# A graph network's edge loop that takes the nodes' end along, 46 of 49 pairs of node tiles

## The chip, the cores and the metric
One core of one Trainium2 chip. The metric is device time in microseconds of one execution. The core's engines are PE (matrix products), DVE (vector), ACT (scalar functions), POOL and SP; SP only issues DMAs here, and POOL issues indirect ones (gathers).

## The reference
12500 nodes of 64 values and 412500 edges, sorted by destination (400000 random ones in both directions and one loop a node, 33 edges a node on the average). Cut to what matters:
```python
x = layernorm(x + mean_over_neighbours_3_times(x))
xs, xr = x[src], x[dst]
flux_send = einsum(mlp_flux(xs).reshape(E, 64, 2), nvec)
flux_recv = einsum(mlp_flux(xr).reshape(E, 64, 2), nvec)
a = mlp_a((xs + xr) * 0.5)            # 3 hidden layers with relu, linear, layernorm
flux = 0.5 * (flux_send + flux_recv) - 0.5 * a * (xs - xr)
x = layernorm(x + (x + segment_sum(flux, dst)))
```

## The kernel before
The program runs in stages: preparation (find_nodes), three averaging layers (first_layer, later_layers), node_rows, which computes for each node what depends on the node alone and writes it as a row of 260 values (node_table, T5: x, y, the two flux rows), the edge loop (edge_pass), and the nodes' end (finish).

**The edge loop** takes 1024 edges a step (HE; 8 tiles of 128, TL), 403 steps (HS), with buffers in rings of 8 (RB). POOL gathers the sources' rows, one indirect DMA for a tile of 128 edges, 8 a step (L1635). ACT takes y out of the rows (L1721), PE turns it (L1652, L1655) and runs the layers, ACT applies relu, DVE and ACT the norm, and PE sums by destination (L1686 to L1695): each half step of 512 edges falls into a window of at most 32 nodes, with the last node's partial sum carried over. ACT copies the sums out (L1750), SP stores them to node_sums (ACC) in HBM (L1596), each store waiting for the one before it to land. A step is a software pipeline written out by hand: in the same step c each engine works on chunks c, c - 1, ... c - 5. DVE's step is spread(c) (edge_sel_t and three edge_sel, the selections) and then scale(c - 5) (edge_zx, edge_ssq, edge_sel_r). ACT's ends with root(c - 4), the square root for which the reciprocal and edge_sel_r of DVE's step c + 1 wait. SP's step is: a store of chunk c - 8, a wait for PE's turn of chunk c - 4, the loads of step c (edge_et with the indices, L1605, for POOL and DVE; edge_near, L1607; two edge_yd, L1609), and the other store of chunk c - 8. The order on each engine's queue is the order in which this code is written; nothing is scheduled by a planner. chunks() writes 11 steps in a row and then a loop of 8 steps a turn, 49 turns.

**The end** (finish) works on 98 tiles of 128 nodes in 7 groups of 14 (JG, NG). SP loads the four sums and the node's own row of a group (L1865, L1867, two buffers), DVE combines them in 13 operations (L1895 to L1910) and normalises (layer_norm, L1292 to L1299, with a root on ACT, L1880), SP writes the group out (L1871, L1873). It starts when the edge loop has ended on all engines.

## Time and profile before
| | us |
|---|---|
| median of 3 runs | 7836.83 (7833.52 to 7843.65) |
| the profiled execution | 7838.55 |
| its span | 7836.7 |
| PE, DVE, ACT, POOL busy | 5910.6, 3335.9, 2816.6, 5380.7 |
| edge loop, first to last gather | 3494.6 to 7615.0 |
| the end, first issue to the span's end | 7663.2 to 7836.7 |

The page's slices show the stages: the averaging layers up to 3400 us, with PE and POOL busy; from there the edge loop, in which POOL stands at 7 tenths and DVE at 3 to 4; in the last slice DVE alone. Read a share of busy time by stage only, and for POOL look also at the idle time before its instructions: POOL's issuing of a gather counts as busy, what lies between two of them doesn't.

### The profile page before, as it was taken

How to read it: one execution, taken by the hardware profiler on the slowest of the kernel's cores; microseconds unless marked ns; L12 is line 12 of the kernel's file. 1: busy time of each engine (PE TensorE's matmuls, PEld its weight loads, DVE VectorE, ACT ScalarE, POOL GpSimd, SP SyncE). 2: the span in 40 equal slices, each digit the busy share in tenths (PEclk: the TensorE clock that was granted, in tenths of full speed). 3: DMA queues.
4: the chain of work that ended last, by engine and by line, in shares of the span. 5: the costliest groups of instructions: out<-in, count | busy, mean ns of one | idle time of the engine just before them, and what ended most of it. 6: DMA issues, size and time to landing. Idle time of an engine off the chain costs nothing. (4 is left out here: it accounts for less than half of the span.)

```text
span 7836.7 us, 213920 instructions
## 1 busy us (share of the span) xinstructions
PE 5910.6 (75%) x80407; PEld 4886.7 (62%) x80407; DVE 3335.9 (43%) x6012; ACT 2816.6 (36%) x5153; POOL 5380.7 (69%) x5216
## 2 busy tenths in 40 slices
PE   0159999999999999757777777777777777777770
PEld 0159999989999999524555555555555555555550
DVE  5469989952221111463333333333333333333337
ACT  0168888850000000113444333343333434433440
POOL 5776766647776777217777777777777777777760
PEclk9999999999999999768888888888888888888885
DMA  5234434346665566325555555555555555555545
GB/s 118 73 114 146 145 129 145 130 176 226 215 228 212 206 216 219 114 86 132 137 138 136 136 136 137 137 137 136 136 136 137 138 136 137 137 136 136 137 120 153
DMA packets 647894, 1155.36 MB, mean 147 GB/s; under 512 B 396199, under 2 KB 454503, under 8 KB 629524
## 3 DMA queue, kind: packets, MB, share of 16 engines
q0 software_dynamic: 217440, 521.49, 26.8%
q1 hardware_dynamic: 419168, 593.46, 23.1%
q10 hardware_dynamic: 10212, 25.35, 1.0%
q8 instruction: 765, 12.53, 0.6%
q14 instruction: 309, 2.53, 0.1%
HBM read 931.86 MB, written 207.96 MB: 145 GB/s over the span
## 5 line engine op out<-in xcount | busy, mean ns | idle before, releaser
L1635 POOL DMA_INDIRECT edge_rows<-node_table,edge_et x3224 | 3137.7, 973 | 983.0 <-issue 944.6
L798 POOL DMA_INDIRECT two_rows<-x_parts,src_at x1120 | 1085.3, 969 | 477.8 <-issue 371.9
L1079 PE MATMUL two_acc<-x_parts,two_win 128*128 128x192 bf16 x16072 | 1355.8, 247 | 32.2 <-DMA two_win<-adjacency 16.8
L1079 PEld LDWEIGHTS two_acc<-x_parts,two_win 128*128 128x128 fp8e4 x16072 | 1340.8, 99 | 35.8 <-issue 33.6
L1822 DVE TENSOR_TENSOR edge_zx<-edge_zp,edge_rows 128x512 f32<-128x512 f32 x403 | 278.9, 692 | 2142.3 <-ACT edge_z L1734 2086.5
L1663 PE MATMUL edge_mp<-edge_h,edge_W 128*128 128x512 f32 x1612 | 1124.7, 837 | 0.0
L978 ACT ACTIVATE one_win<-one_count 128x784 fp8e4<-128x784 f32 x1312 | 1073.8, 824 | 135.2 <-PE one_count L939 63.9
L798 POOL DMA_INDIRECT one_rows<-x_parts,src_at x560 | 834.8, 1491 | 335.1 <-PE one_edge_acc L1002 170.4
L1721 ACT ACTIVATE edge_yc<-edge_rows 128x512 f32<-128x512 f32 x403 | 254.0, 630 | 2213.0 <-DMA edge_rows<-node_table,edge_et 2213.0
L1695 PE MATMUL edge_seg<-edge_seg,edge_edge_now 128*1 128x66 f32 x6448 | 292.4, 228 | 839.9 <-ACT edge_seg L1750 839.2
L925 PE MATMUL one_acc<-x_parts,one_win 128*128 128x192 bf16 x8036 | 858.5, 246 | 0.5 <-ACT one_win L978 0.5
L1686 PE MATMUL edge_seg<-edge_rows,edge_sel 128*32 128x66 f32 x6448 | 795.7, 222 | 1.3 <-DVE edge_sel_r L1828 1.2
L1690 PE MATMUL edge_seg<-edge_rows,edge_sel 128*32 128x66 f32 x6448 | 787.4, 221 | 0.0
L1688 PE MATMUL edge_seg<-edge_z,edge_sel_r 128*32 128x66 f32 x6448 | 766.7, 233 | 0.0
L1687 PE MATMUL edge_seg<-edge_rows,edge_sel 128*32 128x66 f32 x6448 | 766.7, 233 | 0.0
L1689 PE MATMUL edge_seg<-edge_zx,edge_sel_r 128*32 128x66 f32 x6448 | 766.6, 233 | 0.0
L1652 PE MATMUL edge_tp<-ident,edge_yc 128*128 128x128 f32 x1612 | 529.3, 349 | 280.7 <-issue 197.6
L939 PE MATMUL one_count<-one_high,one_low 128*128 128x196 bf16 x5248 | 677.4, 250 | 52.2 <-DVE one_high L910 24.6
L1695 PEld LDWEIGHTS edge_seg<-edge_seg,edge_edge_now 128*1 128x1 f32 x6448 | 128.0, 81 | 895.1 <-ACT edge_seg L1750 893.7
L925 PEld LDWEIGHTS one_acc<-x_parts,one_win 128*128 128x128 fp8e4 x8036 | 685.3, 97 | 1.1 <-issue 0.7
L1663 PEld LDWEIGHTS edge_mp<-edge_h,edge_W 128*128 128x128 f32 x1612 | 394.1, 270 | 319.7 <-issue 319.5
L910 DVE TENSOR_TENSOR one_high<-values,one_slot 128x3136 bf16<-128x3136 bf16 x328 | 585.2, 1784 | 0.0
(289 smaller groups left out, 10477.3 us busy)
## 6 DMA issues: line engine op xcount, KB each, us to landing
two_win<-adjacency SPq DMA_DIRECT2D x82, 3136.0 KB
adjacency<-one_win SPq DMA_DIRECT2D x41, 3136.0 KB
edge_near<-near_ids SPq DMA_DIRECT2D x403, 192.0 KB
edge_rows<-node_table,edge_et POOLq DMA_INDIRECT x3224
node_sums<-edge_seg SPq DMA_DIRECT2D x806, 33.0 KB
two_rows<-x_parts,src_at POOLq DMA_INDIRECT x1120
end_sums<-node_sums SPq DMA_DIRECT2D x7, 1848.0 KB
edge_yd<-y_parts SPq DMA_DIRECT2D x806, 12.0 KB
```

The lines of the kernel that those rows point to most:

```text
L798: pool.indirect_dma_start(rows[:, b % 2, i * GB + d, :], None, XP.rearrange("p (j c) -> (p j) c", c=3 * C), bass.IndirectOffsetOnAxis(ap=s ...
L925: mm = pe.matmul(acc[h.b2][:, half * 3 * C:(half + 1) * 3 * C], win[:, h.b2, half, j, :].bitcast(FP8), now[:, j, :], start=(j == 0), stop= ...
L939: mm = pe.matmul(to, low[:, k, 2 * g + i // 2, :, i % 2], high[:, k, 2 * g + i // 2, :, i % 2], start=True, stop=True)
L978: act.activation(to, count[s % 2][:, :, 0:4 * J].rearrange("p b (n v) -> p v b n", n=2), ACT.Copy, saturate=True).then_inc(taken, 1)
L1079: mm = pe.matmul(acc[b][:, half * 3 * C:(half + 1) * 3 * C], win[:, b, half, j, :].bitcast(FP8), now[:, j, :], start=(j == 0), stop=(j == ...
L1635: pool.indirect_dma_start(rows[:, h.b, t, :], None, T5, bass.IndirectOffsetOnAxis(ap=et[:, h.b, 0, t:t + 1].bitcast(I32), axis=0))\
L1663: pe.matmul(mp[i - 1][:, :], W[:, i - 1, :], hT[i - 1][:, h.b % 2, :], start=True, stop=True)\
L1686: pe.matmul(into(0), sel[:, h.b, 1, t, :], row[:, X_F0:X_F0 + W6], start=first, stop=False, tile_position=(0, 0))
L1687: pe.matmul(into(1), sel[:, h.b, 0, t, :], row[:, 0:W6], start=first, stop=False, tile_position=(0, NW))
L1688: pe.matmul(into(2), sel_r[:, h.b % 2, t, :], z[:, h.b % 2, t, :], start=first, stop=False, tile_position=(0, 2 * NW))
L1689: pe.matmul(into(3), sel_r[:, h.b % 2, t, :], zx[:, h.b % 2, t, :], start=first, stop=False, tile_position=(0, 3 * NW))
L1690: pe.matmul(into(0), sel[:, h.b, 2, t, :], row[:, X_F1:X_F1 + W6], start=False, stop=False, tile_position=(0, 0))
```

## The change
Most tiles of nodes are complete long before the edge loop ends, since the edges are sorted by destination. The change moves the end of 92 of the 98 tiles into the loop, as 46 pairs, one pair per turn of 8 steps.

SP, ACT and DVE now write 35 steps in a row (chunks with more = 3), and their loop has 46 turns; PE and POOL keep 11 steps and 49 turns. In the loop, a pair goes through the 8 steps ("turn" 0 to 7) thus. SP in turn 0: loads the pair's sums and own rows, behind the step's second store. DVE in turns 1, 2 and 3: 4, 4 and 5 operations of combine, on 128 columns; in turn 4 mean, difference, squares and their sum. ACT in turn 5: a square root. DVE in turn 6: reciprocal and product. SP in turn 7: waits for these and writes 256 rows out. DVE's part stands at the end of its step, behind edge_sel_r, and ACT's behind its last root. Pair k is loaded when the stores of chunks up to 26 + 8k have landed. find_nodes gets a test that pair k's edges end before the step 27 + 8k (four small operations and an addition); where they don't, the program takes its general path, which also serves other unusual inputs. finish handles the last 6 tiles in two groups of 3. Two broadcast loads (the norm's factors) come ahead of two others in the edge loop's set-up on SP.

```diff
+DONE_LAG = 3
+DONE = (HS - RB - (HS - RB) % RB - DONE_LAG * RB) // RB
+DONE_PEEL = RB + (HS - RB) % RB + DONE_LAG * RB
+JE = (J - 2 * DONE) // 2
...
-def chunks(eng, body, total=CH, ring=NB):
-
-    peel = ring + (total - ring) % ring
+def chunks(eng, body, total=CH, ring=NB, more=0):
+
+    peel = ring + (total - ring) % ring + more * ring
...
+            pool.iota(done_by[:, :], pattern=[[RB * HE, DONE]], base=(DONE_PEEL - RB) * HE, channel_multiplier=0,
...
+            o.link(dve.tensor_tensor(late, start[0:1, 2:2 * DONE + 2].rearrange("p (k i) -> p k i", i=2)[:, :, 0], done_by[:, :], ALU.subtract))
+            o.link(dve.tensor_reduce(span_gap[:, 0:1], late, AX, ALU.max))
+            o.link(dve.tensor_scalar(span_gap[:, 0:1], span_gap[:, 0:1], 0.0, None, ALU.is_gt))
+            o.link(dve.tensor_copy(late[:, 0:1], span_gap[:, 0:1]))
...
+            sp.dma_start(alw_b[:, :], alw.partition_broadcast(P)).then_inc(L, 16)
+            sp.dma_start(alb_b[:, :], alb.partition_broadcast(P)).then_inc(L, 16)
...
+                if not early(h, DONE_PEEL):
+                    turn = (h.place - DONE_PEEL) % RB
+                    if turn == 0:
+                        sp.wait_ge(sems["stored"], (h.c - BACK) * 2 * 16)
+                        sp.sem_inc(sems["storing"], 1)
+                        sp.wait_ge(sems["done_used"], h.r + 1)
+                        sp.sem_inc(sems["storing"], 1)
+                        sp.dma_start(node_sums[:, :, :, :].rearrange("p j k c -> p j (k c)"),
+                                     ACC.rearrange("(j p) k c -> p j (k c)", p=P)[:, bass.ds(2 * h.r, 2), :]).then_inc(sems["done_in"], 16)
+                        sp.dma_start(own[:, :, :], T5.rearrange("(j p) c -> p j c", p=P)[:, bass.ds(2 * h.r, 2), :]).then_inc(sems["done_in"], 16)
+                    elif turn == 7:
+                        sp.wait_ge(sems["done_made"], h.r + 1)
+                        sp.sem_inc(sems["storing"], 1)
+                        sp.dma_start(out[bass.ds(2 * P * h.r, 2 * P), :].rearrange("(j p) c -> p j c", p=P), res[:, :, :]).then_inc(sems["done_out"], 16)
+            chunks(sp, step, HS, RB, DONE_LAG)
             for c in range(HS - BACK, HS):
                 for u in range(2):
                     store(Chunk(0, c, RB), u)
             sp.wait_ge(sems["stored"], 2 * HS * 16)
+            sp.wait_ge(sems["done_out"], DONE * 16 + 16)
...
+                if not early(h, DONE_PEEL) and (h.place - DONE_PEEL) % RB == 5:
+                    act.wait_ge(sems["done_squares"], h.r + 1)
+                    act.activation(done_stat[:, :], done_stat[:, :], ACT.Sqrt, bias=eps4_col[:, 0:1], scale=1.0 / C)\
+                        .then_inc(sems["done_rooted"], 1)
 
             stages = ((1, lambda h: relu(h, 0)), (2, lambda h: relu(h, 1)), (3, lambda h: relu(h, 2)), (4, squares), (5, take), (4, root))
-            chunks(act, step, HS, RB)
+            chunks(act, step, HS, RB, DONE_LAG)
...
+            oc = Chain(dve, sems["order_c"])
+
+            def done(h, turn):
+
+                x1 = own[:, :, 0:C]
+                wide = lambda col: col.broadcast_to([P, 2, C])
+                each = lambda rw: rw.unsqueeze(1).broadcast_to([P, 2, C])
+                own_cnt = cnt[:, bass.ds(2 * h.r, 2)].unsqueeze(2)
+                if turn == 1:
+                    oc.at(h.r * 20)
+                    dve.wait_ge(sems["done_in"], 32 * h.r + 32)
+                    dve.wait_ge(sems["done_out"], 16 * h.r + 16)
+                    oc.link(dve.tensor_tensor(res[:, :, :], own[:, :, X_F0:X_F0 + C], wide(node_sums[:, :, 0, C:C + 1]), ALU.mult))
+                    oc.link(dve.tensor_tensor(mix[:, :, :], own[:, :, X_F1:X_F1 + C], wide(node_sums[:, :, 0, C + 1:C + 2]), ALU.mult))
+                    oc.link(dve.tensor_tensor(res[:, :, :], res[:, :, :], node_sums[:, :, 0, 0:C], ALU.add))
+                    oc.link(dve.tensor_tensor(res[:, :, :], res[:, :, :], mix[:, :, :], ALU.add))
+                elif turn == 2:
+                    oc.link(dve.tensor_tensor(mix[:, :, :], x1, node_sums[:, :, 2, 0:C], ALU.mult))
+                    oc.link(dve.tensor_tensor(mix[:, :, :], node_sums[:, :, 3, 0:C], mix[:, :, :], ALU.subtract))
+                    oc.link(dve.tensor_tensor(mix[:, :, :], mix[:, :, :], each(alw_b[:, :]), ALU.mult))
+                    oc.link(dve.tensor_tensor(res[:, :, :], res[:, :, :], mix[:, :, :], ALU.subtract))
+                elif turn == 3:
+                    oc.link(dve.tensor_tensor(mix[:, :, :], x1, wide(own_cnt), ALU.mult))
+                    oc.link(dve.tensor_tensor(mix[:, :, :], node_sums[:, :, 1, 0:C], mix[:, :, :], ALU.subtract))
+                    oc.link(dve.tensor_tensor(mix[:, :, :], mix[:, :, :], each(alb_b[:, :]), ALU.mult))
+                    oc.link(dve.tensor_tensor(res[:, :, :], res[:, :, :], mix[:, :, :], ALU.subtract))
+                    oc.link(dve.scalar_tensor_tensor(res[:, :, :], x1, 4.0, res[:, :, :], ALU.mult, ALU.add))
+                    dve.sem_inc(sems["done_used"], 1)
+                elif turn == 4:
+                    spread_of = lambda col: col.unsqueeze(2).broadcast_to([P, 2, C])
+                    oc.link(dve.tensor_reduce(done_mean[:, :], res[:, :, :], AX, ALU.add))
+                    oc.link(dve.tensor_scalar(done_mean[:, :], done_mean[:, :], 1.0 / C, None, ALU.mult))
+                    oc.link(dve.tensor_tensor(res[:, :, :], res[:, :, :], spread_of(done_mean[:, :]), ALU.subtract))
+                    oc.link(dve.tensor_tensor(done_sq[:, :, :], res[:, :, :], res[:, :, :], ALU.mult))
+                    oc.link(dve.tensor_reduce(done_stat[:, :], done_sq[:, :, :], AX, ALU.add))
+                    dve.sem_inc(sems["done_squares"], 1)
+                elif turn == 6:
+                    spread_of = lambda col: col.unsqueeze(2).broadcast_to([P, 2, C])
+                    dve.wait_ge(sems["done_rooted"], h.r + 1)
+                    oc.link(dve.reciprocal(done_stat[:, :], done_stat[:, :]))
+                    oc.link(dve.tensor_tensor(res[:, :, :], res[:, :, :], spread_of(done_stat[:, :]), ALU.mult))
+                    dve.sem_inc(sems["done_made"], 1)
+
             def step(h):
                 spread(h)
                 if not early(h, LAG):
                     scale(h.back(LAG))
-            chunks(dve, step, HS, RB)
+                if not early(h, DONE_PEEL):
+                    done(h, (h.place - DONE_PEEL) % RB)
+            chunks(dve, step, HS, RB, DONE_LAG)
...
+    JG, NG, J0 = JE, 2, 2 * DONE
...
-        res = sb("res", [P, J, C])
+        res = sb("res", [P, J - J0, C])
...
+                js = slice(J0 + g * JG, J0 + (g + 1) * JG)
...
```

**DVE, end of a step in the loop.** Before, edge_sel_r (L1828) is followed by the next step's selections:
```order
L1827 RECIPROCAL edge_ssq<-edge_ssq 128x8
L1828 TENSOR_TENSOR edge_sel_r<-edge_sel,edge_ssq 128x256
L1803 REGISTER_ALU
L1804 TENSOR_SCALAR edge_sel_t<-edge_near,edge_node_of 96x1024
L1809 TENSOR_TENSOR edge_sel<-edge_ramp,edge_et 128x256
L158 REGISTER_ALU
L1810 TENSOR_TENSOR edge_sel<-edge_sel,edge_et 128x256
L1811 TENSOR_TENSOR edge_sel<-edge_sel,edge_et 128x256
```
After, in turn 2, the pair's four operations stand between (L1870 is L1828 of before, L1846 is L1804):
```order
L1869 RECIPROCAL edge_ssq<-edge_ssq 128x8
L1870 TENSOR_TENSOR edge_sel_r<-edge_sel,edge_ssq 128x256
L1890 TENSOR_TENSOR edge_mix<-edge_own,edge_node_sums 128x128
L163 REGISTER_ALU
L1891 TENSOR_TENSOR edge_mix<-edge_node_sums,edge_mix 128x128
L163 REGISTER_ALU
L1892 TENSOR_TENSOR edge_mix<-edge_mix,edge_alw 128x128
L163 REGISTER_ALU
L1893 TENSOR_TENSOR edge_res<-edge_res,edge_mix 128x128
L163 REGISTER_ALU
L1845 REGISTER_ALU
L1846 TENSOR_SCALAR edge_sel_t<-edge_near,edge_node_of 96x1024
```
edge_sel_t and the three edge_sel of the next step come behind the pair's operations; the step's delivery to PE, edge_sel_r, stays ahead of them.

**SP, end of a step in the loop.** Before, the second store of a step (L1596) is followed by the next step's first:
```order
L1585 ISA
L1585 TENSOR_LOAD edge_base_i
L1585 ISA x2
L1596 ISA
L1596 DMA node_sums<-edge_seg 4x32x66
L1589 ISA
L1594 REGISTER_ALU
```
After, in turn 0, two loads stand between:
```order
L1605 ISA
L1605 TENSOR_LOAD edge_base_i
L1605 ISA x2
L1616 ISA
L1616 DMA node_sums<-edge_seg 4x32x66
L1637 REGISTER_ALU
L1639 ISA
L1639 DMA edge_node_sums<-node_sums 128x2x264
L1641 ISA
L1641 DMA edge_own<-node_table 128x2x260
L1609 ISA
L1614 REGISTER_ALU
```
The next step's store and its loads, edge_et among them, come behind these. In turn 7 the output of the pair stands in the same place, behind a wait for DVE.

**DVE, the end.** Before, the groups have 896 columns (14 tiles of 64):
```order
L1885 MEMSET end_eps_col 128x1
L1895 TENSOR_TENSOR end_res<-end_own,end_sums 128x896
L1896 TENSOR_TENSOR end_am<-end_own,end_sums 128x896
L1897 TENSOR_TENSOR end_res<-end_res,end_sums 128x896
L1898 TENSOR_TENSOR end_res<-end_res,end_am 128x896
```
After, 192 (3 tiles):
```order
L1973 MEMSET end_eps_col 128x1
L1983 TENSOR_TENSOR end_res<-end_own,end_sums 128x192
L1984 TENSOR_TENSOR end_am<-end_own,end_sums 128x192
L1985 TENSOR_TENSOR end_res<-end_res,end_sums 128x192
L1986 TENSOR_TENSOR end_res<-end_res,end_am 128x192
```
The operations of a group and their order are the same; there are 2 groups instead of 7.

## Rows read from the trace of the kernel before

**Rows 1.** Busy time by stretch: stretch, its length, each engine, clock, DMA
```profile
3700.00:7600.00 3900.00, 2894.23 (x46199) 2056.39 (x46197) 1365.11 (x3429) 1559.10 (x3434) 2969.63 (x3052) 0.84 0.56 137
7663.00:7836.00 173.00, 0.00 (x0) 0.00 (x0) 140.43 (x141) 2.15 (x7) 0.00 (x0) 0.50 0.56 171
```
**Rows 2.** Groups by line, 3700 to 7600 us: count, busy us, mean ns, idle before
```profile
L1635 POOL DMA_INDIRECT edge_rows<-node_table,edge_et x3052 | 2969.9, 973 | 930.6 <-issue 893.7 <-DMA edge_et<-edges_turned 28.4 <-PE edge_seg L1695 8.5
...
L1828 DVE TENSOR_TENSOR edge_sel_r<-edge_sel,edge_ssq 128x256 f32<-128x256 f32 x381 | 162.5, 426 | 13.1
L1810 DVE TENSOR_TENSOR edge_sel<-edge_sel,edge_et 128x256 f32<-128x256 f32 x381 | 162.0, 425 | 13.1
L1811 DVE TENSOR_TENSOR edge_sel<-edge_sel,edge_et 128x256 f32<-128x256 f32 x381 | 161.8, 425 | 0.0
...
L1809 DVE TENSOR_TENSOR edge_sel<-edge_ramp,edge_et 128x256 f32<-128x256 f32 x381 | 157.0, 412 | 0.0
```
**Rows 3.** Waits, 3700 to 7600 us: us in total, times, longest
```profile
ACT edge_yc L1721 <- DMA edge_rows<-node_table,edge_et: 2043.2, 382, 8.0
DVE edge_zx L1822 <- ACT edge_z L1734: 1962.9, 363, 8.4
...
PEld edge_tp L1652 <- issue: 270.0, 329, 5.3
...
SPq L1590 <- ACT edge_seg L1750: 541.4, 228, 5.1
```
**Rows 4.** The gathers' line, 3700 to 7600 us: ns least/middle/most
```profile
L1635 POOL DMA_INDIRECT edge_rows<-node_table,edge_et x3052: 946/950/1525, 3699.7 to 7599.0; - x191
```
**Rows 5.** Timeline of POOL and DVE: start, us, what, idle before
```profile
5511.99 1.10 POOL L1635 DMA_INDIRECT edge_rows<-node_table,edge_et  x1 [0.30 <-issue]
...
5517.17 0.95 POOL L1635 DMA_INDIRECT edge_rows<-node_table,edge_et  x1 [0.30 <-issue]
...
5519.69 0.96 POOL L1635 DMA_INDIRECT edge_rows<-node_table,edge_et  x1 [0.30 <-issue]
...
5512.16 0.42 DVE L1809 TENSOR_TENSOR edge_sel<-edge_ramp,edge_et 128x256 f32<-128x256 f32 x1
...
5517.53 0.69 DVE L1822 TENSOR_TENSOR edge_zx<-edge_zp,edge_rows 128x512 f32<-128x512 f32 x1 [4.15 <-ACT edge_z L1734]
...
5526.27 0.42 DVE L1828 TENSOR_TENSOR edge_sel_r<-edge_sel,edge_ssq 128x256 f32<-128x256 f32 x1
```
**Rows 6.** Groups by line, 900 to 1900 us, the first averaging layer
```profile
L798 POOL DMA_INDIRECT one_rows<-x_parts,src_at x349 | 509.9, 1461 | 226.1 <-PE one_edge_acc L1002 125.1 <-issue 100.9
...
L910 DVE TENSOR_TENSOR one_high<-values,one_slot 128x3136 bf16<-128x3136 bf16 x208 | 371.2, 1785 | 0.0
...
L909 DVE TENSOR_TENSOR one_low<-values,one_slot 128x2048 bf16<-128x2048 bf16 x207 | 252.9, 1222 | 45.5 <-PE one_count L939 38.0 <-DVE x_parts L883 5.7 <-issue 0.4
```
**Rows 7.** The chain that ended last, then the timeline, from 7663 us on
```profile
7664.53 13.88 DMA end_own<-node_table
...
7678.53 1.09 DVE L1895 TENSOR_TENSOR end_res<-end_own,end_sums 128x896 f32<-128x896 f32 x1 [15.23 <-DMA end_own<-node_table]
...
7699.89 1.09 DVE L1895 TENSOR_TENSOR end_res<-end_own,end_sums 128x896 f32<-128x896 f32 x1
...
7828.04 0.37 SPq L1871 DMA_DIRECT2D out<-end_res  x1
```
**Rows 8.** Timeline of the edge loop's set-up, DVE and SP
```profile
3491.95 0.22 DVE L1012 TENSOR_TENSOR edge_bo_rest<-edge_bo_rest,edge_bo_parts 128x64 f32<-128x64 f32 x1
...
3479.95 0.59 SPq L1580 DMA_DIRECT2D edge_bo<-in_L_gnn_a_bo  x1
```
**Rows 9.** Timeline of SP's queue: in the loop, and the tail
```profile
5507.81 0.36 SPq L1605 DMA_DIRECT2D edge_et<-edges_turned  x1
...
5525.09 4.91 SPq L1596 DMA_DIRECT2D node_sums<-edge_seg  x2
...
7640.16 20.15 SPq L1596 DMA_DIRECT2D node_sums<-edge_seg  x7
```

More of the change, by code:

```diff
@@ L97 @@
 assert GC % GB == 0 and BLKS == DP - 1 and DP % 2 == 1 and BLKS % 2 == 0 and PARTS == 5
+DONE_LAG = 3
+DONE = (HS - RB - (HS - RB) % RB - DONE_LAG * RB) // RB
+DONE_PEEL = RB + (HS - RB) % RB + DONE_LAG * RB
+JE = (J - 2 * DONE) // 2
+assert 0 < DONE < PAIRS - 1 and J == 2 * DONE + 2 * JE
 CLEARS = 101
@@ L212, in build_program @@
                        cnt, has, rcnt, end_idx, start_idx, beyond, src_at, near_at)
-        general = nc.values_load(beyond[0:1, 0:1], min_val=0, max_val=4 * P)
+        general = nc.values_load(beyond[0:1, 0:1], min_val=0, max_val=5 * P)
         with nc.If(general == 0):
@@ L458, in find_nodes @@
         tile_low = sb("tile_low", [P, 2 * HQ])
+        done_by, late = sb("done_by", [1, DONE]), flat[0:1, 4 * 2 * HQ * GC:4 * 2 * HQ * GC + DONE]
         e_dst, e_src = sb("e_dst", [RR, 2, HE], I32), sb("e_src", [RR, 2, HE], I32)
@@ L517, in _ @@
         def _(pe):
-            pe.wait_ge(consts, 5)
+            pe.wait_ge(consts, 6)
             for k in range(4):
@@ L744, in _ @@
             o.link(dve.tensor_scalar(past[0:1, :], past[0:1, :], float(SPAN), None, ALU.is_gt))
+            o.link(dve.tensor_tensor(past[0:1, :], past[0:1, :], late[:, 0:1], ALU.add))
             for b in range(2):
@@ L1555, in edge_pass @@
         bh = sb("bh", [P, 3])
+        node_sums, own = sb("node_sums", [P, 2, 4, W6]), sb("own", [P, 2, W5])
+        res, mix, done_sq = sb("res", [P, 2, C]), sb("mix", [P, 2, C]), sb("done_sq", [P, 2, C])
+        done_stat, done_mean, eps4_col = sb("done_stat", [P, 2]), sb("done_mean", [P, 2]), sb("eps4_col", [P, 1])
+        alw_b, alb_b = sb("alw", [P, C]), sb("alb", [P, C])
         tp, zp = ps("tp", [P, 4 * P]), ps("zp", [P, TL, C])
@@ L1611, in step @@
                     store(h.back(BACK), 1)
-            chunks(sp, step, HS, RB)
+                if not early(h, DONE_PEEL):
[13 more added lines that the diff above has]
+            chunks(sp, step, HS, RB, DONE_LAG)
             for c in range(HS - BACK, HS):
@@ L1868, in _ @@
             for g in range(NG):
-                whole = min(JG, J - 1 - g * JG)
+                whole = min(JG, J - J0 - 1 - g * JG)
                 sp.wait_ge(done, g + 1)
-                sp.dma_start(out[g * JG * P:(g * JG + whole) * P, :].rearrange("(j p) c -> p j c", p=P),
+                sp.dma_start(out[(J0 + g * JG) * P:(J0 + g * JG + whole) * P, :].rearrange("(j p) c -> p j c", p=P),
                              res[:, g * JG:g * JG + whole, :]).then_inc(stored, 16)
-            sp.dma_start(out[(J - 1) * P:N, :], res[0:N_LAST, J - 1, :]).then_inc(stored, 16)
+            sp.dma_start(out[(J - 1) * P:N, :], res[0:N_LAST, J - J0 - 1, :]).then_inc(stored, 16)
             sp.wait_ge(stored, 16 * (NG + 1))
@@ L1887, in _ @@
             for g in range(NG):
-                b, js = g % 2, slice(g * JG, (g + 1) * JG)
+                b, js = g % 2, slice(J0 + g * JG, J0 + (g + 1) * JG)
                 dve.wait_ge(brought[b], 32 * (g // 2 + 1))
-                sm, ow, h = sums[:, b, :, :, :], own[:, b, :, :], res[:, js, :]
+                sm, ow, h = sums[:, b, :, :, :], own[:, b, :, :], res[:, g * JG:(g + 1) * JG, :]
                 x1 = ow[:, :, 0:C]
```

16 lines of the change are left out of this document (10 added, 6 removed).

## The prediction
> **What bounds the kernel now.** I read the busy time of the last two stages first [rows 1]. Between 3700 and 7600 us, inside the edge loop, POOL is busy 2970 of 3900 us and everybody else less (DVE 1365, ACT 1559). Behind 7663 only DVE works, 140 of 173 us: that is the nodes' end, 2.2% of the span. Next the loop's groups by line [rows 2]: POOL issues 3052 gathers of 973 ns, and its idle time before them is 931 us, 305 ns apiece, almost all of it "issue", so it waits for nothing that the profile shows. Sum: 2970 + 931 = 3901 us, the whole stretch. POOL sets the loop's pace: 8 gathers a step, 8 x 1.278 = 10.22 us, and 403 steps make the 4.12 ms. The waits confirm it from the other side [rows 3]: ACT waits 2043 us for gathered rows and DVE 1963 us for ACT, 5.2 us of each 10.2 us step; SP's queue waits 541 us for ACT, 1.4 us a step. So the question is twofold: what the 173 us of the end shrink to, and what the work taken along costs POOL.
>
> **What disturbs POOL.** A gather takes 946 ns at least, 950 in the middle and 1525 at most [rows 4]. The excess over the least is 2970 - 3052 x 0.946 = 83 us, 0.22 us a step. The timeline says who it is [rows 5]: the gather at 5511.99 has the DVE operation of 5512.16 on top of it, and the two that follow it, of two SBUF inputs each, and takes 1.10 us; the one at 5517.17, beside the 0.69 us operation that reads one input from PSUM (edge_zx), takes 0.95. The stretch of the first layer shows the same effect large: there the gathers take 1461 ns in the mean, beside two-input operations of 1785 and 1222 ns [rows 6]. The mechanism as I read it: a gather that reads its indices from SBUF while DVE has two SBUF inputs waits until the DVE operation ends.
> The Trainium skill ("SBUF — State Buffer", Who interferes with whom) says that a DVE instruction with two SBUF inputs contends with a GpSimd instruction that reads SBUF; by that rule these waits are expected, and the 1.10 us beside 0.95 us agrees.
>
> **The change part by part.**
> *Removed: the end on DVE.* A group of 14 tiles starts at 7678.53 and the next at 7699.89 [rows 7]: 21.36 us, seven of them 149.5 us, up to the last output's issue at 7828.04. Each has 16 two-input operations (12 of combine, the one with the factor 4, 3 of the norm) of 1.09 us, 1.126 with the step to the next; two reductions of about as much; and 21.36 - 18 x 1.126 = 1.09 us of small ones and the turn to ACT. After it there are two groups of 3 tiles, 192 columns. An operation takes 0.22 us at 64 columns [rows 8], 0.41 to 0.43 at 256 [rows 2] and 1.09 at 896 [rows 7], a straight line of about 1.04 ns a column: 0.354 us at 192, 0.39 with the step. A group: 18 x 0.39 + 1.09 = 8.1 us, two 16.2. **Saved: 149.5 - 16.2 = 133.3.**
> *The end's load.* The first group's rows land at 7678.41, 13.9 us behind their issue [rows 7], with 3.8 MB each for this group and the one behind it under way. Of 3 tiles it is 0.8 MB a group: at the rate seen (3.8 MB in 14 us) 3 us of transfer. The tail's stores follow one another at (20.15 - 0.6) / 6 = 3.26 us, each waiting for the landing of the one before [rows 9], so a latency is below that, an estimated 2 us. I take 5 instead of 14. **Saved: 9** (8 to 11). The last output is smaller too: **0.5** (0 to 2).
> *Added before the loop.* Two broadcast loads on SP ahead of those for which DVE waits, 0.59 us each by the row of a like one [rows 8]: **+1.2**, as POOL's first gather waits for that set-up. Four small operations of the test and an addition in the node search, on DVE, some 0.2 us each: **+0.8** (0 to 1.2). The iota on POOL is under 0.2 us, beside DMAs.
> *Added in the loop, 46 times in 8 steps.* DVE gets 16 two-input operations of 128 columns, 0.29 us each by the line above (4.6 us), two reductions, a scaling and a reciprocal (together 1 us): 5.6 us in 81.8, at most five or six operations and 1.7 us in one step. They stand behind edge_sel_r, where the step's product for PE is already delivered, and ahead of the next selections. DVE waits 5.2 us a step for ACT [rows 3], so their own time costs nothing; without that cover it would be 46 x 5.6 = 258 us. What they cost is POOL's wait. The four two-input operations of a step take 643 us in the stretch [rows 2], 1.69 us a step, and go with 0.22 us of excess: 0.13 us a us. In proportion the new ones cost 4.64 x 0.13 = 0.60 us an iteration; if both the chance to meet a reading gather and the wait grow with the operation's length (0.29 against 0.42), 0.41. The bounds: nothing, if POOL gets its turn in the gaps between short operations; and the ratio of the first layer, where operations are four times as long: (1461 - 946) x 349 = 180 us over 371 + 253 us of DVE [rows 6], 0.29, which makes 1.34 us an iteration, 62 us. I take 0.5, near the row of like length: **+23** (0 to 62).
> *ACT* gets one square root of 2 columns behind its own root, under 1 us by any row, in a step in which it waits 5.2 us for rows: **0**.
> *SP, and who waits behind it.* In turn 0 two loads of 270 KB, each 0.4 to 1 us to issue, behind the step's second store; in turn 7 a wait for DVE and an output of 64 KB. What is queued behind that wait is the next step's store and then edge_et, for which POOL waits. How early is edge_et? The one issued at 5507.81 serves the step whose first gather starts at 5519.69 [rows 9, 5]: 12 us ahead. SP follows PE's turns, and PE is up to 5.3 us late at its branch [rows 3], so some 6.6 us are left at worst, of which landing takes 2 to 3. How late can SP become? It starts its step's last store at 5525.09 and is free at 5525.7; DVE's edge_sel_r of the step before ends at 5526.69 [rows 5], and the pair's last two operations, of turn 6, would end 0.55 us later, at 5527.2; the output's issue takes it to 5528. The row of the two stores ends at 5530.00, so the next store started near 5529.4, with an estimated microsecond of register work ahead of it. So SP is late by 0 to 2 us once in eight steps, and 1.4 us of idle time a step win it back: **0** (0 to 10). The loads' 540 KB may hold gathers and stores by some 2 to 4 us, by the rate above; gathered rows are needed by ACT, and PE's sums free a buffer more than a step before POOL wants it.
> *The tail.* SP's chain of stores is the last thing before the end: seven stores in 20.15 us from 7640.16 [rows 9]. SP enters the tail some 5 us later by the wait in turn 7; the first stores of the tail still go at POOL's pace of 10.2 us for two, against 6.5 us of their own, so this is won back: **0** (0 to 3).
> *The head.* On SP, ACT and DVE 35 steps instead of 11 stand in a row before the loop proper; it is the same work, and each of them waits in every step: **0**.
>
> **The sum.** -133.3 - 9 - 0.5 + 1.2 + 0.8 + 23 = -117.8. The profiled execution has 7836.7 of span and 7838.55 in all, 1.7 above the median of 7836.83; in its own terms the span goes to 7718.9, and on the median it is 7836.8 - 117.8 = **7719**.
>
> **The rivals.**
> 1. *POOL is blocked for the whole of each new operation* (ends on the other side). The place is the index read of the gathers, the price 4.64 us an iteration. If a gather could not go on at all while a two-input operation runs, 46 x 4.64 = 213 us would be added: 7836.8 - 142.8 + 2 + 213 = **7909**. It decides from 142.8 - 2 = 141 us on, 3.06 us an iteration, that is 0.66 us of POOL's time per us of DVE's. Against it: the loop shows 0.13 and even the first layer 0.29. The Trainium skill (the same section) says that whoever comes second is fully blocked until the first has finished; the wait is then the rest of one operation, not its whole length, unless the read always comes at its start. By that rule read strictly the time would be this rival's. For it: the new operations come as chains with 35 ns between them, so that a gather could meet two in a row. Chance 4%.
> 2. *SP starves POOL.* If the wait in turn 7, or the 540 KB ahead of the stores, puts edge_et later than POOL's start, each us of it counts 46 times. With 1 us an iteration the time is 7719 + 46 = **7765**. For it: PE's 5.3 us at the branch, less 3 of landing, leave a lead of only 4. Against: that delay reaches DVE two steps behind the branch (edge_sel_t waits for the turn two steps back), in turn 2, and not in turn 6, for which SP waits. Chance 7%.
> 3. *The work in the loop costs nothing on POOL*: **7696**. For it: POOL wins the gaps. Against: even isolated operations cost it now. Chance 12%.
> 4. *The change does not do what it says*: the new test sends the program down the general path. Pair k needs its last edge by step 27 + 8k; at 33 edges a node it ends at 8448 (k + 1), against 1024 (27 + 8k): for k = 45 388608 against 396288. The margin of 7680 edges is far more than random edges scatter. Chance 1%, at a time far above all ranges.
>
> **How the numbers follow.** The forecast, with 0.3 to 0.8 us an iteration (7710 to 7733), has 76%. With rival 3 and most of rival 2 the range is 7692 to 7762: the lower end is rival 3 with the load's best case and a little of the last output, the upper one the first layer's ratio (7719 + 39 = 7758) and some us of SP. 0.2% are 15.7 us, about what a measurement of this kernel tells from no change. Faster by over 0.2% needs less than 2.7 us an iteration: 94%. Within 0.2%: 1%. Slower: 5% (rivals 1 and 4).
>
> **What would show each step.** Behind the loop: two groups of about 8 us on DVE with operations of 0.35 us, and the first landing 5 us behind its issue. In the loop: POOL's gathers with a mean of 980 to 987 ns instead of 973, the slow ones under the new edge_res and edge_mix operations, 10.25 to 10.35 us a step, and no idle time of POOL for edge_et. SP should wait for DVE 1 to 4 us in turn 7. I am wrong if POOL shows idle time before a gather that ends with edge_et (rival 2), if gathers beside the new operations are slowed by 0.3 us or more each time (rival 1), or if the tail's seven stores take longer than 20 us.

## The result, and the profile after

The changed kernel takes 7723.11 us (median of 4 runs, 7712.23 to 7734.1) against 7835.18 us of the kernel before on the same chip (4 runs, 7819.5 to 7843.65): ratio 0.9859, interval 0.9838 to 0.9881, faster by 1.4%. The forecast was 7719, in a range of 7692 to 7762. The profiled execution of the changed kernel took 7727.65 us, its span 7722.8 us, 113.9 us shorter than the span before.

First the two stretches of [rows 1], after; the columns are the same, and the second stretch is now 57 us long instead of 173:
```profile
3700.00:7600.00 3900.00, 2885.31 (x45874) 2059.58 (x45873) 1598.10 (x4325) 1561.23 (x3458) 2973.75 (x3034) 0.83 0.58 143
7663.00:7720.00 57.00, 11.69 (x377) 10.13 (x373) 19.56 (x56) 6.64 (x19) 0.00 (x0) 0.65 0.14 39
```
In the loop DVE has 233 us more in 3900, and POOL issued 18 gathers fewer in the same time. Behind the loop 20 us of DVE are left of 140.

The groups by line of the same stretch, the counterpart of [rows 2]:
```profile
L1670 POOL DMA_INDIRECT edge_rows<-node_table,edge_et x3034 | 2974.9, 981 | 926.6 <-issue 888.4 <-DMA edge_et<-edges_turned 32.3 <-PE edge_seg L1730 5.8
...
L1846 DVE TENSOR_SCALAR edge_sel_t<-edge_near,edge_node_of 96x1024 bf16<-96x1024 bf16 x379 | 194.0, 512 | 417.0 <-PE edge_tp L1690 257.5 <-DMA edge_near<-near_ids 115.7 <-DVE edge_done_stat L1907 15.4
...
L1851 DVE TENSOR_TENSOR edge_sel<-edge_ramp,edge_et 128x256 f32<-128x256 f32 x379 | 155.9, 411 | 0.0
...
L1898 DVE TENSOR_TENSOR edge_res<-edge_res,edge_mix 128x128 f32<-128x128 f32 x45 | 13.1, 292 | 1.5
...
L1885 DVE TENSOR_TENSOR edge_res<-edge_own,edge_node_sums 128x128 f32<-128x128 f32 x46 | 13.1, 285 | 0.0
```
A gather takes 981 ns in the mean instead of 973, POOL's idle time is still "issue", 305 ns apiece, and its wait for edge_et is 32 us against 28. The new operations take 0.285 to 0.292 us (0.29 forecast). New is edge_sel_t's wait for edge_near, 116 us. The gathers' line shows the least and the middle as in [rows 4]; only the slow ones grew in number:
```profile
L1670 POOL DMA_INDIRECT edge_rows<-node_table,edge_et x3034: 946/954/1547, 3699.6 to 7599.8; - x190
```

Then the end, as in [rows 7]: SP's last stores of the loop and the end's loads, DVE's first operation of each of the two groups, and the outputs.
```profile
7632.50 57.41 SPq L1616 DMA_DIRECT2D node_sums<-edge_seg  x16
...
7694.19 0.49 SPq L1955 DMA_DIRECT2D end_own<-node_table  x1
...
7699.78 0.36 DVE L1983 TENSOR_TENSOR end_res<-end_own,end_sums 128x192 f32<-128x192 f32 x1 [6.83 <-DMA end_own<-node_table]
...
7707.79 8.46 SPq L1959 DMA_DIRECT2D out<-end_res  x2
7707.85 0.36 DVE L1983 TENSOR_TENSOR end_res<-end_own,end_sums 128x192 f32<-128x192 f32 x1
...
7716.29 0.46 SPq L1961 DMA_DIRECT2D out<-end_res  x1
```

With these starts the 113.9 us fall into six parts. The first and the last gather, and the end's first issue on SP (7663.16 and 7692.82), are read from the timelines.

| part of the span | before | after | difference | forecast |
|---|---|---|---|---|
| up to the first gather | 3494.6 | 3497.4 | +2.8 | +2.0 |
| first to last gather | 4119.5 | 4144.6 | +25.1 | +23 |
| last gather to the end's first issue | 49.1 | 50.9 | +1.8 | 0 |
| that issue to DVE's first operation | 15.4 | 7.0 | -8.4 | -9 |
| DVE's groups, to the last output's issue | 149.5 | 16.5 | -133.0 | -133.3 |
| the rest | 8.7 | 6.5 | -2.2 | -0.5 |

So the saving is where it was expected, and 25 of 144 us are given back in the loop. Which mechanism takes them is the open question: the new operations themselves, as the forecast's term says, or the operations behind them, which they push back.

**Who makes the gathers late.** A gather with nothing in its way starts 1.25 us after the one before (0.95 and 0.30). For each gather after which the next is late by x (25 ns or more) I looked for a DVE operation that ends at its start + x + 0.12 us, within 25 ns. Nearly always there is exactly one, and I take it as the one the gather waited for. Summed over the steps of the loop proper (the 46 turns), smaller delays included, x is 81.4 us before and 105.8 after, +24.4, the loop's loss. By turn of the eight steps the rise is in two of them: turn 3 from 16.9 to 29.8 us, turn 4 from 10.2 to 19.5; all the others together 54.3 and 56.5. By the operation at whose end the wait ended (whole loop, us): the first edge_sel 30.5 before and 62.8 after, the second and third 24.7 and 23.4, edge_sel_r 9.6 and 7.3, edge_sel_t 6.3 and 2.6, all the new operations 3.4, in 43 gathers. This place shows both at once (DVE, then POOL):
```profile
4482.98 0.29 DVE L1905 TENSOR_TENSOR edge_res<-edge_res,edge_done_mean 128x128 f32<-128x128 f32 x1
4483.31 0.29 DVE L1906 TENSOR_TENSOR edge_done_sq<-edge_res 128x128 f32<-128x128 f32 x1
4483.63 0.29 DVE L1907 TENSOR_REDUCE edge_done_stat<-edge_done_sq 128x2 f32<-128x128 f32 x1
4484.26 0.48 DVE L1846 TENSOR_SCALAR edge_sel_t<-edge_near,edge_node_of 96x1024 bf16<-96x1024 bf16 x1 [0.34 <-DVE edge_done_stat L1907]
4484.66 0.42 DVE L1851 TENSOR_TENSOR edge_sel<-edge_ramp,edge_et 128x256 f32<-128x256 f32 x1
...
4483.14 0.95 POOL L1670 DMA_INDIRECT edge_rows<-node_table,edge_et  x1 [0.30 <-issue]
4484.39 1.50 POOL L1670 DMA_INDIRECT edge_rows<-node_table,edge_et  x1 [0.30 <-issue]
```
The gather at 4483.14 starts under the new operation of 4482.98, which ends 0.13 us later; two more start while it runs, and it takes its 0.95 us. The next one begins inside edge_sel_t, is not let in when that ends, and goes on only when the first edge_sel ends too, at 4485.08: it takes 1.50 us. edge_sel_t and the first edge_sel stand one behind the other with no gap, a block of 0.82 us. Gathers over 0.3 us late in the loop proper: 13 before, 87 after. The block of turn 4 falls near turn 3's last gather: in the mean it began 1.8 us ahead of that gather's start before the change and begins 0.25 us ahead after. The block of turn 5 began 1.1 us ahead of turn 4's last gather and now begins with it. 39% and 57% of these last gathers are over 0.3 us late now. The waits that end with the first edge_sel rise from 2.0 to 24.1 us at these two gathers, and from 2.3 to 11.7 us at the second and third gather of turn 3.

**What holds a gather.** The three traces before, after and light_gap (below) give the rule plainly. The second and third edge_sel, edge_sel_r and the new two-input operations were already running, for 0.05 us or more, at the start of 598 gathers and ended 0.16 us or more behind it: all 598 gathers were late, 590 of them by that end less 0.12 us, within 30 ns. 1265 times such an operation began 0 to 0.3 us behind a gather's start: not one gather waited for its end. So an operation holds a gather only if it already runs when the gather starts (or is joined to one that does, as below), and the gather loses the operation's rest less 0.12 us. An estimate from this, for gathers 1.25 us apart that meet the operations at random: the 736 new operations of 0.29 us cost 736 x (0.29 - 0.05 - 0.12)^2 / (2 x 1.25) = 4.2 us (3.4 measured); 403 blocks of 0.82 us that held to their end would cost 68 us.

The block does not always hold to its end. Of the gathers that began inside edge_sel_t (0.1 us or more after its start, 0.16 or more ahead of its end), 37 went on at edge_sel_t's own end in the trace before, and 11 at the first edge_sel's; after, it is 14 and 73. The latter cost 5.2 us before and 36.0 after, which is the whole rise at the first edge_sel. It goes by the turn: before, all of turns 0 and 5 (11) were held to the second end and none of the others (30 in the loop proper); after, all 25 of turns 3 and 4 are too. The row of [rows 5] that the prediction reads is of the first kind, as the line that is missing there shows:
```profile
5511.76 0.48 DVE L1804 TENSOR_SCALAR edge_sel_t<-edge_near,edge_node_of 96x1024 bf16<-96x1024 bf16 x1 [4.33 <-PE edge_tp L1655]
```
The gather of 5511.99 took 1.10 us, 0.15 more than the least, and that fits the end of edge_sel_t at 5512.24 less 0.12; the first edge_sel was already running by then. The two kinds have the same overlap of 80 ns between the two operations. In the looped steps of the eight traces without an added wait they separate by one thing: DVE's last register or semaphore instruction ahead of the first edge_sel ended up to 0.151 us after edge_sel_t's start in all 216 of the first kind, and 0.160 us or more after it in all 237 of the second. That is a correlation; no run varied it.

### The profile page after: what moved, and what is told of

Read it like the earlier page. It is cut to its first block and busy times, and to the rows that moved or that the text cites. A ratio compares the mean times of both kernels' runs of the same rounds, so it can differ in the third digit from the quotient of the medians.

```text
span 7722.8 us, 216276 instructions
## 1 busy us (share of the span) xinstructions
PE 5923.9 (77%) x80407; PEld 4903.8 (63%) x80407; DVE 3453.0 (45%) x6838; ACT 2827.7 (37%) x5194; POOL 5394.2 (70%) x5217
## 5 line engine op out<-in xcount | busy, mean ns | idle before, releaser
L1698 PE MATMUL edge_mp<-edge_h,edge_W 128*128 128x512 f32 x1612 | 1105.4, 824 | 0.0
L1687 PE MATMUL edge_tp<-ident,edge_yc 128*128 128x128 f32 x1612 | 556.2, 362 | 318.2 <-issue 234.3
```

The lines of the kernel that those rows point to most:

```text
L1698: pe.matmul(mp[i - 1][:, :], W[:, i - 1, :], hT[i - 1][:, h.b % 2, :], start=True, stop=True)\
```

## The experiments

Theories: A1, the new two-input operations cost POOL directly (the forecast's term); A2, they cost almost nothing, and the block edge_sel_t + edge_sel that they push is what costs; C, SP's lateness.

In four sets of runs every kernel took half as long again in all its stages, the kernel before too (11732 to 11895 us). Most of POOL's idle time is then a wait for edge_et, so the times of these runs can't test A1 against A2; only ratios within a set are used. The changed kernel as it stands is in none of them.

**no_sums, early, gap_after, gap_before** (one set; before 11872.91). no_sums keeps the pair's loads, waits, root and output in the loop and leaves out DVE's arithmetic, early moves done() between spread() and scale() and ACT's root to the start of its step, and gap lets the first edge_sel wait for edge_sel_t's end; gap_before is the kernel before with that wait.
```diff
 no_sums, in done():   - oc.link(dve.tensor_tensor(...))   (all operations of turns 1 to 6)
 early, DVE's step:      spread(h)
                       + if not early(h, DONE_PEEL): done(...)
                         scale(h.back(LAG))
                       - if not early(h, DONE_PEEL): done(...)
 gap:                  - o.at(base + h.c)
                       + o.at(base + 2 * h.c)
                       - dve.tensor_scalar(sel_t[...], near[...], ...)
                       + o.link(dve.tensor_scalar(sel_t[...], near[...], ...))
```


> Leaves the pair's arithmetic on DVE out of the loop (16 two-input operations, reductions, scaling, reciprocal); the loads, the waits, the square root on ACT and the output stay, so 92 tiles are written as zeros. First gather to last gather was 4119.5 us before and 4144.6 with the change. Theory A (the arithmetic's operations stand in POOL's way, themselves or by what they push back): the stretch falls to 4119 to 4124. Theory C (the 540 KB of loads and SP's lateness cost the time): it stays at 4138 to 4147. The time would be about 20 us below the changed kernel's by A, the same by C.

> The pair's part on DVE moves ahead of scale: it stands between spread (edge_sel_t and the three edge_sel) and edge_zx, in DVE's wait for ACT, so that it pushes edge_sel_t no longer back; the square root on ACT moves to the start of its step. The same 16 operations run. Theory A1 (the new operations themselves block gathers, 0.5 us an iteration): first to last gather stays near 4144, within 5. Theory A2 (they cost POOL next to nothing; the loss comes from edge_sel_t and the first edge_sel, pushed to a moment at which a gather starts, in turns 3 and 4): the stretch falls to 4120 to 4128, the time by 15 to 25 us.

> The changed kernel with one wait more in each step: the first edge_sel waits until edge_sel_t has ended, so that there is a gap of some 35 ns between the two. Theory A2: a gather that is held by edge_sel_t gets in at the gap instead of waiting for the end of the first edge_sel as well; of the 58 us that gathers wait up to that end now, some 40 go, and first to last gather falls from 4144.6 to 4100 to 4115. Theory A1: the gap changes nothing, 4140 to 4150.

> The kernel before with the same gap between edge_sel_t and the first edge_sel. Theory A2: of the 28 us that gathers wait up to the end of the first edge_sel in it, about 20 go: first to last gather from 4119.5 to 4096 to 4106. Theory A1: no change, 4117 to 4122.

Measured: no_sums 11634.31, 0.9801 [0.9768, 0.9834]; early 11757.47, 0.9898 [0.9882, 0.9915]; gap_after 11601.04, 0.9761 [0.9725, 0.9797]; gap_before 11878.05, 1.0001 [0.9992, 1.0011]. From first to last gather they have 6759.7, 6883.0, 6740.0 and 6873.3 us, where the kernel before had 4119.5 in its own trace. The groups by line between 5500 and 11000 us say why these times test no theory, first gap_before:
```profile
L1635 POOL DMA_INDIRECT edge_rows<-node_table,edge_et x2563 | 2448.1, 955 | 3052.4 <-DMA edge_et<-edges_turned 2336.7 <-issue 715.7
```
and no_sums, with no new arithmetic at all:
```profile
L1670 POOL DMA_INDIRECT edge_rows<-node_table,edge_et x2604 | 2502.1, 961 | 2996.8 <-DMA edge_et<-edges_turned 2096.2 <-issue 748.9 <-PE edge_seg L1730 98.0
```
POOL is idle for 3000 of 5500 us and waits 2100 to 2300 of them for edge_et, so a gather that is 0.3 us late need not cost anything. What holds there is the end: early has gap_before's loop (+9.7 us) and is 121 us faster, about what the end saved. no_sums and gap_after have a loop that is 114 and 133 us shorter than gap_before's. I have no reason that I could show for that. The single gathers do speak: in no_sums, with edge_sel_t and edge_sel joined, 23 of the 40 that began inside edge_sel_t were held to the first edge_sel's end, the longest took 1533 ns; in gap_after all 43 went on at edge_sel_t's end, and the longest took 1223.

**gap_after2 and early2** (two of these kernels again, in two further sets).


> Again the changed kernel with the gap between edge_sel_t and the first edge_sel, since in the first run of it the program took 1.5 times as long in all its stages, the kernel before too, and POOL was idle for half the loop. Where POOL is never idle, theory A2 expects first to last gather at 4100 to 4115 us instead of 4144.6, and about 30 us less time than the changed kernel (near 0.982 of the kernel before). Theory A1 expects no change: 4140 to 4150, 0.986.

> Again the kernel in which the pair's part on DVE stands between spread and edge_zx, to be read where POOL is never idle. Theory A2 (the 16 operations themselves cost POOL next to nothing, the pushed edge_sel_t does): first to last gather 4120 to 4128 us instead of 4144.6, ratio to the kernel before about 0.983. Theory A1 (the operations themselves block gathers): 4140 to 4150, ratio 0.986.

Measured: 11449.3, 0.9734 [0.9694, 0.9773], and 11601.59, 0.9881 [0.9865, 0.9898]: the slow pace again and the same two ratios.

**The light kernels.** PE does a quarter of its sums by destination (6 of 24 products a half step are left; the 9 of the expectation is a miscount), so that it can't be what sets the pace:
```diff
 in sums(h):   - for k in range(4):
               + for k in range(1):      (quarters 1 to 3 end at their first product)
               - for q in range(4):      (the carried row)
               + for q in range(1):
```
light_before is the kernel before with this edit, light_after the changed one, light_early and light_gap add the edits above to light_after. Their sums are incomplete, so they are only good for timing. One execution each, beside one of the kernel before of 7831.13: the usual pace was back for the whole kernel as well, and on a chip on which early2 had run at the slow one, so it is not the edit that brought it back.

> The kernel before with 9 of 24 products by destination left per half step (one edge tile of four is summed, and one of four carried rows added; the sums are therefore incomplete): in the earlier runs on this chip PE issued its products 1.4 us apart over half of each step and POOL waited. Both theories: with PE out of the way POOL sets the pace again, first to last gather 4100 to 4140 us, gathers at 1.25 us with some slowed. It is the base for the next three.

> The changed kernel with the same products left out. Both theories: the stretch is longer than light_before's by 10 to 30 us (25 in the whole kernels). They differ in which DVE operation's end the slowed gathers wait for: theory A1 expects the 16 new operations, theory A2 the first edge_sel behind edge_sel_t, in turns 3 and 4 of eight.

> The same with the pair's part on DVE between spread and edge_zx. Theory A2: within 6 us of light_before. Theory A1: as light_after.

> light_after with the gap between edge_sel_t and the first edge_sel. Theory A2: below light_after by 20 us or more, and below light_before as well. Theory A1: as light_after.

Measured, with waits by the operation at whose end they ended, as above (us, whole loop):

| | time | first to last gather | first edge_sel | edge_sel_t | new operations | gathers over 0.3 us late, loop proper |
|---|---|---|---|---|---|---|
| light_before | 7836.05 | 4117.9 | 32.8 | 7.0 | - | 25 |
| light_after | 7741.69 | 4165.1 | 83.7 | 2.5 | 5.8 | 133 |
| light_early | 7710.5 | 4136.1 | 36.9 | 4.4 | 5.8 | 19 |
| light_gap | 7683.62 | 4102.7 | 0 | 16.6 | 5.8 | 4 |

light_before repeats the kernel before (7836.05 and 4117.9 us of gathers), so POOL sets the pace here as there; without that the rest would say nothing. The change costs 47.2 us of loop here, where both theories expected 10 to 30, and the waits at the first edge_sel alone rise by 50.9. Of the 133 gathers over 0.3 us late, 74 are in turns 3 and 4, where A2 had them, but 24 in turn 1, where it had none. light_early has the same new operations and the same loads, and leaves the block about where it was: the loss falls to 18.2 us, the first edge_sel to 36.9. So where the pair's operations stand is 29 of 47 us, and A1 alone falls. But A2 had expected light_early within 6 us of light_before; 18 is a miss. Of the 18.2 us, 5.8 are waits that end with a new operation, 6.4 are delays under 25 ns that my reading gives to nobody, and 4.1 are at the first edge_sel; 5.1 of the 18.2 arise in the first 35 steps, where no pair is worked on. These are single executions, and four of the kernel before lie 24 us apart: the 18 us are not clear of that, the 29 barely, and it is the sort of the waits that bears the reading.

light_early changes a second thing. DVE's part comes earlier in its step, so that SP waits for it less in turn 7, and edge_et is issued 10.4 us ahead of turn 0's first gather in the mean, against 6.0 in light_after. By itself the pair light_after and light_early could not tell A2 from C. light_gap can: SP is as late in it as in light_after (6.3 us ahead), and its loop is the shortest.

light_gap breaks the block. Its groups by line between 3900 and 7600 us, POOL and the first edge_sel:
```profile
L1670 POOL DMA_INDIRECT edge_rows<-node_table,edge_et x2907 | 2812.3, 967 | 888.8 <-issue 852.3 <-DMA edge_et<-edges_turned 28.3 <-PE edge_seg L1730 8.2
...
L1851 DVE TENSOR_TENSOR edge_sel<-edge_ramp,edge_et 128x256 f32<-128x256 f32 x363 | 158.5, 437 | 29.9 <-DVE edge_sel_t L1846 19.7 <-issue 0.5 <-PE edge_seg L1730 0.2
```
against light_after:
```profile
L1670 POOL DMA_INDIRECT edge_rows<-node_table,edge_et x2861 | 2824.9, 987 | 875.4 <-issue 836.5 <-DMA edge_et<-edges_turned 27.7 <-PE edge_seg L1730 11.2
```
967 ns a gather instead of 987, less than the 973 of light_before, with all the new operations in place. The timeline shows the gap, 0.21 us between edge_sel_t and edge_sel (35 ns were expected), and gathers beside it at 1.04 and 1.13 us:
```profile
5288.79 0.48 DVE L1846 TENSOR_SCALAR edge_sel_t<-edge_near,edge_node_of 96x1024 bf16<-96x1024 bf16 x1 [0.33 <-DVE edge_done_stat L1907]
5289.48 0.42 DVE L1851 TENSOR_TENSOR edge_sel<-edge_ramp,edge_et 128x256 f32<-128x256 f32 x1 [0.21 <-DVE edge_sel_t L1846]
...
5289.05 1.04 POOL L1670 DMA_INDIRECT edge_rows<-node_table,edge_et  x1 [0.30 <-issue]
5290.40 1.13 POOL L1670 DMA_INDIRECT edge_rows<-node_table,edge_et  x1 [0.30 <-issue]
```
Over the whole loop the longest gather of light_gap is 1266 ns:
```profile
L1670 POOL DMA_INDIRECT edge_rows<-node_table,edge_et x3224: 946/955/1266, 3499.2 to 7601.9; - x190
```
That of light_after is 1547:
```profile
L1670 POOL DMA_INDIRECT edge_rows<-node_table,edge_et x3224: 946/950/1547, 3494.0 to 7659.1; - x190
```
The loop is 62.4 us shorter than light_after's and 15.2 shorter than light_before's, the program 58 us shorter. The sum closes: light_before less its 32.8 us at the first edge_sel, plus 9.6 more at edge_sel_t and 5.8 of new operations, is 4100.5; measured 4102.7. All 128 gathers that began inside edge_sel_t went on at its end, where it was 14 of 122 in light_after. The 62 us are well clear of the spread of single executions, the 15 are not; for them speaks only that the sum closes.

**gap_after3 and gaps_two** (one set; before 11894.88). gaps_two also breaks the second edge_sel from the third:
```diff
 - o.at(base + 2 * h.c)
 + o.at(base + 3 * h.c)
 - dve.tensor_tensor(sel[:, h.b, 1, :, :], ...)
 + o.link(dve.tensor_tensor(sel[:, h.b, 1, :, :], ...))
```


> The whole changed kernel with the gap between edge_sel_t and the first edge_sel, once more. The runs with fewer products gave 4165.1 us without and 4102.7 with the gap. Where POOL is never idle: theory A2 expects first to last gather 4095 to 4115 us instead of 4144.6, a time of about 7723 - 35 = 7688, ratio to the kernel before 0.981. Theory A1: 4140 to 4150, ratio 0.986.

> The same with a second gap, between the second and the third edge_sel, which now run in one block of 0.77 us. Theory A2: the waits up to the third one's end (about 9 us in all) mostly go; 4 to 10 us less than with one gap, ratio 0.980. Theory A1: no difference from the changed kernel.

Measured, at the slow pace once more: gap_after3 11589.33, 0.9748 [0.9732, 0.9765]; gaps_two 11603.15, 0.9759 [0.9737, 0.9781]. The second gap brings nothing there, where POOL is not what bounds the loop, so this does not test what was expected of it. The changed kernel with the gap has the lowest median in each set in which it ran, 2.4 to 2.7% under the kernel before, though its interval overlaps those of no_sums and gaps_two. At the usual pace the whole version was not run. The light pair says 58 us; as the waits at the first edge_sel are 62.8 us in the whole kernel against 83.7 in the light one, some 45 us is my estimate for it.

## Why the prediction came out

The time was right (7719 against 7723), and the terms of the end within a microsecond or two. The loop's term was right in its number and wrong in its cause: that it hit was luck.

- **The end.** Groups 8.07 us apart (8.1 forecast), operations of 0.36 us (0.354), 16.5 us in all (16.2): the straight line through 0.22 us at 64 columns, 0.41 at 256 and 1.09 at 896 held at 192. The load landed so that DVE began 7.0 us behind SP's first issue instead of 15.4; 8.4 saved, 9 forecast, the term that mixed a rate with an estimated latency. The rest gave 2.2 where 0.5 (0 to 2) was set, just outside.
- **The head.** +2.8 against +2.0: 1.2 up to the edge loop's first load, 1.6 in its set-up. Right in size.
- **The loop's term, +23.** It was written as 46 iterations x 4.64 us of new two-input operations x 0.11, as if any such operation cost POOL in proportion to its length. Measured is +25.1, of which waits at the new operations themselves are 3.4 us: 0.016 us per us of theirs (5.8 us and 0.027 in the light kernels). The other 21 come from where edge_sel_t and the first edge_sel now stand: +32.3 at the first edge_sel, and 11 less at the others and in small delays. The step that failed is "four two-input operations take 643 us and go with 83 us of excess, 0.13 a us": a mean over operations that stand alone and a block of two, and with edge_sel_t, the block's first, not counted. By the count and the estimate above the cost of an operation does not go with its length, but with the square of what it has beyond 0.17 us. The clue was in [rows 5]: the gather of 1.10 us was put down to the three edge_sel on top of it, but all three start behind it; what it waited for is edge_sel_t, which the rows leave out. The second clue, that DVE's order puts edge_sel_t behind the pair's operations, I had described and priced at nothing, "their own time costs nothing", because DVE has 5.2 us of idle time. That cover is real for DVE and PE; POOL is not under it. It cares when the block comes, not whether DVE has time.
- **Rival 1** (blocked for the whole of each operation, 7909): wrong, by 3.4 us instead of 213. The gather at 4483.14 takes 0.95 us under two new operations. By the Trainium skill ("SBUF — State Buffer", Who interferes with whom) whoever issues first holds the shared ports for the whole instruction and the other is fully blocked. For a gather that comes second the row of 4484.39 agrees, and so do the 598 above, with 0.12 us of the wait costing nothing. The other way round the runs differ: a new operation that starts while a gather runs is not held by it (0.290 us in the mean, 0.295 for those that start between gathers), nor does it hold the gather. That is why a chain of short operations on top of a gather costs it so little, as at 4483.14.
- **Rival 3** (no cost, 7696): wrong in the result, near in the mechanism. In light_gap, with a gap in the block, the loop is 15 us shorter than light_before's even with the new work in it, in one execution of each.
- **SP and rival 2.** The forecast was a delay of 0 to 2 us, won back at once. Worked out over all steps of the loop proper, edge_et's issue led its step's first gather by 9.8 to 11.5 us in every turn before; after it leads by 6.2, 6.4, 6.9, 7.8, 8.3, 9.4, 10.2 and 10.6 us in turns 0 to 7, 4.6 at least. So SP is 4.5 us late at turn 0 and needs the eight steps to win it back: size and recovery were both off. Its wait for DVE in turn 7 is 3.2 us, within the 1 to 4 of the forecast; but the next store starts 4.8 us behind the output's issue in the mean, where the forecast had 1.4. The wait (3800 to 7600 us), then the rows behind it (SP's queue, turn 7 and turn 0):
```profile
SPq L1644 <- DVEq L1914: 142.4, 45, 5.1
...
3928.18 0.44 SPq L1645 DMA_DIRECT2D out<-edge_res  x1
3933.23 0.68 SPq L1616 DMA_DIRECT2D node_sums<-edge_seg  x1
3934.34 0.36 SPq L1625 DMA_DIRECT2D edge_et<-edges_turned  x1
3938.94 0.65 SPq L1616 DMA_DIRECT2D node_sums<-edge_seg  x1
3940.01 0.41 SPq L1639 DMA_DIRECT2D edge_node_sums<-node_sums  x1
3940.65 0.39 SPq L1641 DMA_DIRECT2D edge_own<-node_table  x1
```
  The edge_et of 3934.34 serves the gathers from 3939.41 on, 5.1 us ahead, and landing is within that. POOL's wait for edge_et stays at 32 us, so rival 2 did not come. By the prediction's 2 to 3 us for landing, which no row shows, the least lead of 4.6 us leaves some 2 us to spare. DVE feels it first: edge_sel_t waits 116 us for edge_near, issued behind edge_et, mostly in turns 0 and 1, and begins 0.7 to 0.9 us later in them relative to the gathers. These have 3.7 us more of excess in the two turns (14.6 before, 18.3 after). So C is worth a few us at the most, and light_gap agrees.
- **The tail.** +1.8 against 0 (0 to 3); SP's last seven stores take 20.1 us, as before.

What stays open: why light_early keeps 18 us where the new operations account for 5.8; the share of placement in the full kernel, which rests on the reading of its trace and on the light pair, since no full run at the usual pace moved the block; what makes a gather slip in between edge_sel_t and the first edge_sel in some turns and not in others; and why at the slow pace the loops of no_sums and gap_after are some 120 us shorter than those of early and gap_before.

## What to carry to other kernels

When an engine can hold up the one that sets the pace, idle time on it is no licence to shift its work: look at which operations stand back to back and which instruction of the bounding engine will now start under them, turn by turn. A price per microsecond taken as a mean over short and joined operations can hit the sum and miss the cause; sort the slow instructions by the operation at whose end their wait ends before extrapolating, and ask of each operation whether it ran when they started. If two operations in a row hold the other engine, a wait between them (0.21 us here, 62 us won over the loop in the light pair) can be cheaper than any reordering.

## What the runs showed of the hardware

- An indirect gather of 128 rows is held by a DVE operation with two SBUF inputs, and by edge_sel_t as well, which has one tensor input in SBUF, in bf16: in light_gap 130 gathers wait to its end, 16.6 us in all. The Trainium skill (the same section) lists tensor_scalar among the operations that can take both port pairs, under conditions, and the runs agree that this one holds a gather; whether by the pairs, no run separates.
- The operation must already be running when the gather starts: 598 of 598 gathers were late then, by the operation's rest less 0.12 us, and none of 1265 waited for one that began 0 to 0.3 us behind its start (before, after and light_gap). edge_zx, with one input in PSUM and one in SBUF, ran at the start of 440 gathers in these traces and held none.
- Back to back, edge_sel_t and the first edge_sel can act as one block: a gather that begins in the first is held to the end of the second (1.50 us) in 73 of 87 cases after, but in 11 of 48 before. With 0.21 us between them it never is (1266 ns at most over a whole loop).
- Two-input operations of 0.29 us, 35 ns apart, cost the gathers 0.016 us per us of theirs in the changed kernel, 0.027 in the light ones.
- The whole program took half as long again in four sets of runs, on three chips, with a mean granted clock of 0.75 to 0.77 instead of 0.88 to 0.89. On one of these chips it later ran at the usual pace. The cause isn't known, and the clock alone, 14% lower, doesn't explain 50%.
